# A macaron block in float32 on one core: y is normalised into a buffer in SBUF, GpSimd makes its low part, and the order of the work is written anew

## The chip, the cores and the metric

The kernel runs on one core of one Trainium2 chip. The metric is the device time of one execution in microseconds (us), the median over several executions. Less is better.

## The reference

x has 16 sequences of 1024 tokens with 512 channels. Three sublayers follow one another, each on the layer norm of its input:

```
x = x + 0.5 * ffn(layernorm(x))
x = x + attn(layernorm(x))
x = x + 0.5 * ffn(layernorm(x))

ffn(x):  s = x @ Win + bin                    # 512 -> 64
         h = relu(s[..., None] * W1 + b1)     # 64 -> 64 x 16
         g = sum(h * W2, -1) + b2             # back to 64
         return g @ Wout + bout               # 64 -> 512
attn(x): q, k, v = split(x @ w_attn)          # 16 heads of 32
         q, k = elu(q) + 1, elu(k) + 1
         S_t = S_{t-1} + k_t v_t^T;  z_t = z_{t-1} + k_t
         y_t = (q_t S_t) / (q_t . z_t + 1e-6)
         return y @ w_proj
```

## The kernel before, in words

The tokens are cut into NB = 32 blocks of 512, four tiles of 128 tokens each; two blocks make a sequence. Block j of the main loop does the attention of block j and, packed into the two halves of the partitions, the last feed-forward of block j-1 (half 0) and the first feed-forward of block j+2 (half 1). Blocks -2 and -1 before the loop and NB and NB+1 behind it are feed-forwards that run alone.

Products with large weights are made in three passes (`split3`): a float32 operand is a high part, rounded to the format that TensorE takes at full rate, and a low part, the rest. High parts are made by a copy on ScalarE (ACT), low parts by a subtraction, mostly on VectorE (DVE). For y, the attention's output, these are `yh` (ACT `ysplit`) and `yl` (DVE `ysplit`, in the helper at L931).

In a block the PE program is: `project` (k and q, 96 matmuls), `values`, `key` (a transpose of k), `den`, `ff_in`, and then for the four tiles t: `scores(t)` into the four PSUM banks `att`; ACT copies heads 0 and 2 into `A` and GpSimd (POOL) masks them, DVE masks heads 1 and 3 while it moves them; `attend(t)` adds the state's part (L1501) and the scores' part (L1510) into the same four banks; `update(t)` (L1521) makes the state's increment; DVE `ynorm(t)` divides y by its denominator in place in `att`; ACT and DVE split it; `outer(t)`, two times six matmuls with w_proj, gives what is added to x. `channels` transposes the next block's normalised input, and `ff_out` ends the two feed-forwards. `hidden` is one of 16 steps of a feed-forward's inner sum: a Relu on ACT, and a multiply and add on DVE.

Three things set the order. Each engine's program is a list written out by hand, and an engine runs its list strictly in order. Waits are on semaphores: `take` and `take_all` on PE wait until the bank they are given is free. And which bank a product gets is worked out by `give` when the program is built: the bank among those allowed that was given out longest ago, to be taken when `emptied` says so. ATT are banks 0 to 3 (`att`), RING is banks 5 to 7; bank 4 holds the feed-forward's sum. The banks of scores(t) come free, for scores(t+1) among others, with the semaphore `s_yl`: behind the last reading of y, the DVE subtraction.

Ahead of the loop the weights are loaded into buffers that are free then (`kT`, `qT`, `v`, `A`, `ktok`), and split by ACT and POOL. `s_walo` counts the low parts; DVE's first running sum of k (`zsum`, L1000) writes `A`, so it waits until w_proj's low part has been made from there.

## Time and profile before

| | |
|---|---|
| median of 3 runs | 2327.67 us (2326.47 to 2327.98) |
| the profiled execution: its time | 2329.01 us |
| its span in the trace | 2327.3 us |
| PE busy | 2266.8 us, 97% |
| DVE busy | 1935.2 us, 83% |
| ACT busy | 1438.7 us, 62% |
| POOL busy | 846.0 us, 36% |
| mean granted clock of TensorE | 0.989 |

Busy times are sums over an engine's instructions. A row of the timeline gives the start and the length of an instruction, or of several alike in a row (x4), and in brackets for how long the engine had been idle before it and who released it. PEld is TensorE's loading of weights, which overlaps its matmuls. Matmuls overlap one another, so the cost of one is best read as the distance of the starts.

### The profile page before, as it was taken

To read this page: it belongs to the slowest core of one execution; us is meant where nothing else is said; L and a number is where in the kernel's file an instruction comes from. 1 tells how busy PE (TensorE), PEld (TensorE's weight loads), DVE (VectorE), ACT (ScalarE), POOL (GpSimd) and SP (SyncE) were. 2 spreads that over 40 slices of the span, in tenths; PEclk is the share of its full clock that TensorE was granted. 3 is DMA by queue.
4 is the path that set the end of the run, shared out by engine and by line. 5 is a ranking of instruction groups with operands and counts; after the bars stand their busy time and mean duration, and the time that the engine had idled before them with its cause. 6 is when DMAs were issued, how large, how long until landed. Compare 5 with 4: busy or idle time off the path is not lost.

```text
span 2327.3 us, 74160 instructions
## 1 busy us (share of the span) xinstructions
PE 2266.8 (97%) x32210; PEld 1770.7 (76%) x32210; DVE 1935.2 (83%) x3393; ACT 1438.7 (62%) x2310; POOL 846.0 (36%) x871
## 2 busy tenths in 40 slices
PE   5899999999999999999999999999999999999997
PEld 3677777777777777777777777777777777777775
DVE  6888888889888889888889888889888889887767
ACT  6755657555657556657556656556656656666556
POOL 6333333433243433333333243434234333333312
PEclk8999999999999999999999999999999999999997
DMA  6001101111101111101111111111111111111111
GB/s 179 20 21 38 56 21 57 57 56 38 57 21 57 56 57 38 57 21 57 57 57 38 45 32 57 57 54 41 39 39 57 57 50 45 39 39 38 39 32 44
DMA packets 50215, 111.62 MB, mean 48 GB/s; under 512 B 8801, under 2 KB 10849, under 8 KB 45794
## 3 DMA queue, kind: packets, MB, share of 16 engines
q1 hardware_dynamic: 49890, 106.87, 15.1%
q8 instruction: 254, 4.16, 0.7%
q14 instruction: 71, 0.58, 0.1%
HBM read 72.25 MB, written 34.60 MB: 46 GB/s over the span
## 4 chain that ended last, share of the span: by engine, by line
PE 79%; DVE 13%; POOL 3%; issue 3%; ACT 2%; DMA 0%; DVEq 0%; SPq 0%; POOLq 0%; ACTq 0%
PE bank L1370 33%; PE att L1370 18%; PE att L1407 6%; PE att L1485 5%; PE att L1510 5%; PE att L1427 3%; DVE st L901 2%; DVE acc_psum L963 2%; PE att L1501 2%; PE bank L1436 2%; PE bank L1473 2%; POOL A L449 1%; DVE yl L931 1%; PE bank L1453 1%; DVE res L976 1%
## 5 line engine op out<-in xcount | busy, mean ns | idle before, releaser
L567 ACT ACTIVATE xhat<-res,nmr,rstd 128x512 f32<-128x512 f32 x384 | 298.4, 809 | 324.9 <-DVE nmr L909 266.7
L588 ACT ACTIVATE ffr<-ffs,b1c,w1c 128x512 f32<-128x512 f32 (+3 forms) x576 | 437.9, 781 | 27.9 <-DVE acc_psum L963 21.7
L453 POOL TENSOR_SCALAR_AFFINE_SELECT A<-A 128x512 f32<-128x512 f32 x256 | 156.6, 635 | 724.1 <-ACT A L540 724.1
L963 DVE SCALAR_TENSOR_TENSOR acc_psum<-ffr,w2c,acc_psum 128x512 f32<-128x512 f32 (+3 forms) x540 | 385.4, 714 | 32.4 <-ACT ffr L588 7.5
L442 POOL TENSOR_TENSOR res<-res,hbout 128x512 f32<-128x512 f32 x256 | 353.9, 1403 | 0.4 <-ACT xhat L567 0.4
L449 POOL TENSOR_TENSOR A<-qT,A 128x512 f32<-128x512 f32 x128 | 192.3, 1514 | 244.6 <-DVE zc L1005 102.2
L901 DVE BATCH_NORM_STATS2 st<-res 128x6 f32<-128x512 f32 x384 | 261.5, 681 | 9.5 <-DMA res<-in_L_attn_x_dram 3.7
L1370 PE MATMUL att<-xh,wa_h 128*128 128x512 f32 x648 | 260.4, 402 | 1.5 <-DVE xl L931 1.5
L1370 PE MATMUL att<-xh,wa_l 128*128 128x512 f32 x648 | 256.7, 396 | 0.0
L1370 PE MATMUL att<-xl,wa_h 128*128 128x512 f32 x648 | 256.7, 396 | 0.0
L1370 PE MATMUL bank<-wa_h,xh 128*128 128x512 f32 x512 | 218.7, 427 | 0.0
L1370 PE MATMUL bank<-wa_h,xl 128*128 128x512 f32 x512 | 202.8, 396 | 0.0
L1370 PE MATMUL bank<-wa_l,xh 128*128 128x512 f32 x512 | 202.8, 396 | 0.0
L540 ACT ACTIVATE A<-att 128x512 f32<-128x512 f32 x256 | 138.3, 593 | 90.9 <-PE att L1485 90.8
L415 POOL TENSOR_SCALAR nmr<-mv 128x4 f32<-128x4 f32 x93 | 21.2, 228 | 458.9 <-DVE mv L903 458.9
L1370 PE MATMUL bank<-wp_h,yh 128*128 128x512 f32 x384 | 171.3, 446 | 0.0
L1025 DVE TENSOR_TENSOR A<-att,tri 128x512 f32<-128x512 f32 x256 | 163.5, 680 | 0.1
L944 DVE STREAM_TRANSPOSE xf<-xhat 128x512 f32<-128x512 f32 x244 | 162.7, 686 | 0.9 <-ACT xhat L567 0.9
L1485 PEld LDWEIGHTS att<-qT,kT 32*128 32x128 f32 x4096 | 125.9, 186 | 38.2 <-DVE yl L931 26.0
L1485 PE MATMUL att<-qT,kT 32*128 32x128 f32 x4096 | 150.3, 283 | 3.6 <-DVE yl L931 3.3
L1370 PEld LDWEIGHTS att<-xh,wa_h 128*128 128x128 f32 x648 | 122.0, 188 | 41.4 <-issue 8.2
L1370 PE MATMUL bank<-wp_l,yh 128*128 128x512 f32 x384 | 152.5, 397 | 1.0 <-issue 1.0
(135 smaller groups left out, 5060.6 us busy)
## 6 DMA issues: line engine op xcount, KB each, us to landing
xf<-scratch SPq DMA_DIRECT2D x128, 256.0 KB, 4.3
res<-in_L_attn_x_dram SPq DMA_DIRECT2D x31, 1024.0 KB, 5.3
out_dram<-res SPq DMA_DIRECT2D x31, 1024.0 KB, 4.3
scratch<-rden SPq DMA_DIRECT2D x128, 8.0 KB, 1.7
res<-in_L_attn_x_dram SPq DMA_DIRECT2D x4, 256.0 KB, 3.7
kT<-in_L_attn_w_attn_dram SPq DMA_DIRECT2D x1, 1024.0 KB, 5.7
qT<-in_L_attn_w_attn_dram SPq DMA_DIRECT2D x1, 1024.0 KB, 9.6
v<-in_L_attn_w_attn_dram SPq DMA_DIRECT2D x1, 1024.0 KB, 12.0
```

The costliest lines, as they stand in the source:

```text
L442: eng.tensor_tensor(r[:, t, :], r[:, t, :], hbout[:, :], ALU.add).then_inc(s_bias[half], 1)
L449: eng.tensor_tensor(z[:, g, :], qT[:, g, :], z[:, g, :], ALU.mult).then_inc(s_zq, 1)
L453: eng.affine_select(out=A[:, h, :, :], in_=A[:, h, :, :], compare_op=ALU.is_ge, fill=0.0, base=0, pattern=[[0, 4], [1, P]], channel_multip ...
L567: eng.activation(xhat[t % 2][:, :], res[b % SLOTS][:, t, :], ACT.Identity, bias=nmr[:, n, b % 2, t:t + 1], scale=rstd[:, n, b % 2, t:t + 1 ...
L588: eng.activation(ffr[i % 2][p, w], ffs[p, w], ACT.Relu, bias=b1c[p, i:i + 1], scale=w1c[p, i:i + 1]).then_inc(s_hr, 1)
L901: eng.bn_stats(st[:, n, o, t, :], r[:, t, :]).then_inc(s_bn[n], 1)
L944: eng.transpose(xf[half][:, t, :, :].rearrange("p c i -> p (c i)"), xhat[t % 2][:, :]).then_inc(s_tr[half], 1)
L963: eng.scalar_tensor_tensor(psum[p, w], r[p, w], w2c[p, i:i + 1], psum[p, w], ALU.mult, ALU.add).then_inc(s_hm, 1)
L1025: eng.tensor_tensor(A[:, h, :, :], att[:, h, :].rearrange("p (g i) -> p g i", g=4), tri[:, :].unsqueeze(1).to_broadcast([P, 4, P]), ALU.mu ...
L1370: op = eng.matmul(o, l, r, start=first and i == 1, stop=final and i == n)
L1407: op = eng.matmul(att[M * n:M * n + M, r, 0:P], win[d, c, :], xf[n][d, :, c, :], start=c == 0, stop=c == C // D - 1)
L1485: op = eng.matmul(att[:, h, g * P:g * P + P], kT[d, g, w], qT[d, g, w], start=True, stop=True)
```

## The change

1. **y in SBUF.** `ynorm` writes into a new buffer `yn` (one, 128x512) and no longer in place. ACT's `ysplit` reads `yn` for the high part, POOL's new `ysplit` makes the low part as `yn` less high part; DVE's is gone. `ynorm(t)` waits in addition until the low part of the tile before has been made.
2. **Banks.** The scores' banks come free with `s_yn`, that is behind `ynorm`.
3. **Order in a block.** On PE `scores(1)` comes ahead of `values(3)`, and each `outer` comes about a tile later; the lists of ACT, DVE and POOL and the calls of `give` are written anew to go with it. POOL runs its four `zsum` together.
4. **Ahead of the loop.** The loads of the five small parameters (ten issues, each parameter into both halves of the partitions) go from SP's queue to ACT's; weights are loaded earlier and in another order; k's, q's and Wout's high parts are made by POOL; low parts are made in pieces of 128x512, so that norms come between them; bout is loaded into all partitions and halved by POOL, where a matmul and an ACT copy did that.
5. **Lone feed-forwards** use four half buffers for the Relu's output, where they had two.

```diff
+        yn = sb("yn", [P, 4, P])
...
-            return {"v": s_v, "xT": s_xTl, "y": s_x2, "sc": s_yl}[kind], 4 * b + i + 1
+            return {"v": s_v, "xT": s_xTl, "y": s_x2, "sc": s_yn}[kind], 4 * b + i + 1
...
             give_all("sc", j, 0)
-            give(RING, ("v", j, 2), ("up", j, 0), ("key", j, 1), ("v", j, 3))
+            give(RING, ("v", j, 2), ("up", j, 0), ("key", j, 1), ("xT", j + 1, 0))
             give_all("sc", j, 1)
-            give(RING, ("xT", j + 1, 0), ("y", j, 0), ("up", j, 1), ("key", j, 2))
+            give(RING, ("v", j, 3), ("key", j, 2), ("y", j, 0))
             give_all("sc", j, 2)
-            give(RING, ("y", j, 1), ("up", j, 2), ("xT", j + 1, 1))
+            give(RING, ("up", j, 1), ("up", j, 2), ("y", j, 1), ("xT", j + 1, 1))
             give_all("sc", j, 3)
-            give(RING, ("y", j, 2))
+            give(RING, ("xT", j + 1, 2), ("xT", j + 1, 3))
...
+            def ysplit(b, t):                                     # POOL
+                o = t % 2
+                e.wait_ge(s_yh, 4 * b + t + 1)
+                eng.tensor_tensor(yl[o][:, :, :], yn[:, :, :], f32(yh[o][:, :, :]), ALU.subtract).then_inc(s_yl, 1)
...
-                copy(yh[o][:, :, :], att[:, :, 0:P], s_yh)        # ACT
+                copy(yh[o][:, :, :], yn[:, :, :], s_yh)
...
                 e.wait_ge(s_num, 4 * b + t + 1)                   # DVE
                 e.wait_ge(s_rs, 64 * (b + 1))
-                eng.tensor_tensor(att[:, :, 0:P], att[:, :, 0:P], rs[:, :, t * P:t * P + P], ALU.mult).then_inc(s_yn, 1)
+                e.wait_ge(s_yl, 4 * b + t)
+                eng.tensor_tensor(yn[:, :, :], att[:, :, 0:P], rs[:, :, t * P:t * P + P], ALU.mult).then_inc(s_yn, 1)
...
-            def ysplit(b, t):                                     # DVE
-                o = t % 2
-                e.wait_ge(s_yh, 4 * b + t + 1)
-                lo_part(yl[o][:, :, :], att[:, :, 0:P], yh[o][:, :, :], s_yl)
...
-                e.wait_ge(s_hm, hid(j, i) - 2)
+                e.wait_ge(s_hm, hid(j, i) - (4 if alone(j) and i >= 2 else 2))
```

Three places in the middle of the loop show what moved. First PE, from `attend(1)` of a block to `attend(2)`. L1501 and L1510 are attend, L1521 is update, L1473 is key, L1485 is scores, wp_h and wp_l are outer. Before:

```order
L1501 MATMUL att<-qT,S 32x128 [waits s_ac1,s_am3,s_am1,s_ac0]
...
L1510 MATMUL att<-A,v 32x128 [waits s_am2,s_am0]
...
L1521 MATMUL bank<-v,ktok 32x32 [waits s_v]
...
L1370 MATMUL bank<-wp_h,yh 128x512
...
L1473 MATMUL bank<-ident,kT 128x128 [waits s_xTl]
...
L1485 MATMUL att<-qT,kT 128x128 [waits s_yl]
...
L1370 MATMUL bank<-wp_h,yh 128x512 [waits s_x2]
```

The same stretch in the changed kernel, where the lines are L1515 and L1524 (attend), L1535 (update) and L1499 (scores):

```order
L1515 MATMUL att<-qT,S 32x128 [waits s_ac1,s_am3,s_am1,s_ac0]
...
L1524 MATMUL att<-A,v 32x128 [waits s_am2,s_am0]
...
L1384 MATMUL bank<-wp_h,yh 128x512 [waits s_yl,s_xTl]
...
L1499 MATMUL att<-qT,kT 128x128 [waits s_yn]
...
L1535 MATMUL bank<-v,ktok 32x32 [waits s_v]
...
L1384 MATMUL bank<-wp_h,yh 128x512
```

Before, half of outer(0), update(1), the other half and a key stood between attend(1) and scores(2), and scores waited on `s_yl`; now only half of outer(0) stands there, scores waits on `s_yn`, and it is outer that waits on `s_yl`.

Second POOL, from the masks of tile 0 to those of tile 3 in a block (L453 is a mask, L442 adds the bias to x). Before:

```order
L453 AFFINE_SELECT A<-A 128x512 [waits s_ac1]
L442 TENSOR_TENSOR res<-res,hbout 128x512 x4
L453 AFFINE_SELECT A<-A 128x512 [waits s_ac0]
L453 AFFINE_SELECT A<-A 128x512 [waits s_ac1]
...
L415 TENSOR_SCALAR nmr<-mv 128x4 [waits s_ag1]
```

And in the changed kernel (L463 is a mask, L447 the bias, L459 the new low part):

```order
L463 AFFINE_SELECT A<-A 128x512 [waits s_ac0]
L463 AFFINE_SELECT A<-A 128x512 [waits s_ac1]
L459 TENSOR_TENSOR yl<-yn,yh 128x512 [waits s_yh]
L447 TENSOR_TENSOR res<-res,hbout 128x512 x2
L459 TENSOR_TENSOR yl<-yn,yh 128x512 [waits s_yh]
L463 AFFINE_SELECT A<-A 128x512 [waits s_ac0]
L463 AFFINE_SELECT A<-A 128x512 [waits s_ac1]
L447 TENSOR_TENSOR res<-res,hbout 128x512
L463 AFFINE_SELECT A<-A 128x512 [waits s_ac0]
L463 AFFINE_SELECT A<-A 128x512 [waits s_ac1]
L459 TENSOR_TENSOR yl<-yn,yh 128x512 [waits s_yh] x2
```

The low part of tile 0 stands behind the masks of tile 1, that of tile 1 behind two biases and ahead of the masks of tile 2, those of tiles 2 and 3 behind the masks of tile 3.

Third ACT in the changed kernel, from the low end of tile 1 to the norm of the next block's tile 1 (L561 is a copy, L609 a hidden, L588 a norm):

```order
L561 ACTIVATE yh<-yn 128x512 [waits s_po,s_yn]
L561 ACTIVATE A<-att 128x512 [waits s_sc0,s_num]
L609 ACTIVATE ffr<-ffs,b1c,w1c 128x512 [waits s_hm]
L561 ACTIVATE A<-att 128x512 [waits s_sc2]
L609 ACTIVATE ffr<-ffs,b1c,w1c 128x512 [waits s_hm]
L561 ACTIVATE ktok<-bank 128x512 [waits s_up,s_kt]
L588 ACTIVATE xhat<-res,nmr,rstd 128x512 [waits s_tr1]
```

Before, the two copies of the scores of tile 2 followed each other directly, as here:

```order
L540 ACTIVATE yh<-att 128x512 [waits s_po,s_yn]
L540 ACTIVATE A<-att 128x512 [waits s_sc0,s_num]
L540 ACTIVATE A<-att 128x512 [waits s_sc2]
L588 ACTIVATE ffr<-ffs,b1c,w1c 128x512 [waits s_hm]
L540 ACTIVATE ktok<-bank 128x512 [waits s_up,s_kt]
```

A `hidden` now stands between the two copies.

## Rows read from the trace of the kernel before

**Rows 1.** The page: the row of ACT's hidden, all forms together.
```profile
L588 ACT ACTIVATE ffr<-ffs,b1c,w1c 128x512 f32<-128x512 f32 (+3 forms) x576 | 437.9, 781 | 27.9 <-DVE acc_psum L963 21.7
```

**Rows 2.** Windows: busy time of each engine, instructions, PEclk, DMA share, GB/s.
```profile
0.00:41.00 41.00, 15.15 (x78) 9.88 (x78) 26.54 (x65) 23.31 (x35) 23.57 (x43) 0.79 0.83 247
41.00:130.00 89.00, 80.87 (x936) 62.27 (x936) 71.88 (x130) 60.29 (x94) 36.26 (x30) 0.94 0.07 17
1393.00:1463.00 70.00, 69.62 (x1014) 54.41 (x1014) 59.35 (x103) 43.22 (x69) 24.61 (x27) 1.00 0.16 48
```

**Rows 3.** Waits of PEld in one block, 1393 to 1463: total, times, longest.
```profile
PEld att L1485 <- DVE yl L931: 0.7, 3, 0.4
```

**Rows 4.** Timeline of PE in that block: attends, outers, scores, feed-forward's end.
```profile
1431.76 0.50 PE L1501 MATMUL att<-qT,S 32*32 32x128 f32 x32
...
1433.09 0.48 PE L1521 MATMUL bank<-v,ktok 128*32 128x32 f32 x32
...
1438.40 0.48 PE L1370 MATMUL bank<-wp_h,yh 128*128 128x512 f32 x1
...
1439.98 0.50 PE L1501 MATMUL att<-qT,S 32*32 32x128 f32 x32
...
1444.85 0.50 PE L1370 MATMUL bank<-wp_h,yh 128*128 128x512 f32 x1
...
1446.59 0.51 PE L1501 MATMUL att<-qT,S 32*32 32x128 f32 x32
...
1453.09 0.51 PE L1501 MATMUL att<-qT,S 32*32 32x128 f32 x32
...
1454.67 0.66 PE L1436 MATMUL bank<-ident,xhat 128*128 128x128 f32 x4
...
1460.23 0.50 PE L1427 MATMUL att<-wo_h,yh 64*128 64x512 f32 x2 [0.25 <-DVE yl L931]
```

**Rows 5.** Chain of waits of that block in order of time: start, us, what.
```profile
1396.45 5.60 PE bank L1370 x24
...
1448.18 0.71 DVE att L1018
...
1448.91 0.60 ACT yh L540
...
1449.54 0.69 DVE yl L931
```

**Rows 6.** Timeline of POOL, DVE and ACT in that block.
```profile
1431.36 5.05 POOL L442 TENSOR_TENSOR res<-res,hbout 128x512 f32<-128x512 f32 x4
...
1433.84 0.69 DVE L1018 TENSOR_TENSOR att<-att,xf 128x512 f32<-128x512 f32 x1
...
1444.99 1.09 ACT L540 ACTIVATE A<-att 128x512 f32<-128x512 f32 x2 [2.10 <-PE att L1485]
...
1445.66 1.22 POOL L453 TENSOR_SCALAR_AFFINE_SELECT A<-A 128x512 f32<-128x512 f32 x2 [5.63 <-ACT A L540]
```

**Rows 7.** Timeline of DVE: two running sums of one block.
```profile
1406.02 1.26 DVE L1000 TENSOR_TENSOR_SCAN A<-kT,zc 128x512 f32<-128x512 f32 x1
...
1410.20 2.07 DVE L1000 TENSOR_TENSOR_SCAN A<-kT,zc 128x512 f32<-128x512 f32 x1
```

**Rows 8.** Timeline of the start, 0 to 56 (SPq is SyncE's issuing of loads).
```profile
7.41 2.07 PE L1537 MATMUL att<-ktok,tri 1*128 1x512 f32 x2 [7.41 <-DMA ktok<-in_L_ffn_bout_dram]
...
6.43 1.24 SPq L357 DMA_DIRECT2D w1c<-in_L_ffn_W_dram  x2
...
18.32 0.63 ACT L540 ACTIVATE wo_h<-ktok 128x512 fp32r<-128x512 f32 x1
...
49.00 4.63 POOL L427 TENSOR_TENSOR wp_l<-A,wp_h 128x2048 fp32r<-128x2048 f32 x1
...
54.99 1.23 DVE L909 SCALAR_TENSOR_TENSOR nmr<-mv,rstd 128x4 f32<-128x4 f32 x1 [5.78 <-POOL rstd L417]
```

**Rows 9.** Timeline of the end: the last feed-forward's sum.
```profile
2314.23 6.78 DVE L963 SCALAR_TENSOR_TENSOR acc_psum<-ffr,w2c,acc_psum 128x128 f32<-128x128 f32 x15
```

More of the change, by code:

```diff
@@ L201, in carried, with relu_of @@
             return 4 * (b // PER * (PER - 1) + b % PER) + g + 1
+        def relu_of(j, i):
+            w = columns(j)
+            o = BLK // 2 * (i // 2 % 2) if alone(j) else 0
+            return ffr[i % 2][halves(j), w.start + o:w.stop + o]
         def hid(j, i):
@@ L369, in _ @@
             load(2)
-            wp_v = w_proj.rearrange("(g h e) n -> g e h n", g=4, h=4)
-            for g in range(4):
-                eng.dma_start(wp_st[D * g:D * g + D, :, :], wp_v[g]).then_inc(s_wp, 16)
             load(3)
@@ L499, in _ @@
                     rstds(L2, 1)
-                if on(j + 2):
-                    bias(1, j + 2, 2)
+                if on(j):
+                    mask(j, 1, 0)
+                    mask(j, 1, 2)
+                    ysplit(j, 0)
                 if on(j - 1):
@@ L504, in _ @@
                     bias(0, j - 1, 2)
[L505 removed]
                 if on(j):
[L507 to L508 removed]
+                    ysplit(j, 1)
                     mask(j, 2, 0)
@@ L1237, in _ @@
                 if on(j):
+                    mask(j, 3, 3)
+                    mask(j, 3, 1)
+                if on(j + 1):
+                    channels(j + 1, 1)
+                if on(j):
+                    outer(j, 1)
+                if j == NB - 1:
+                    var_of(L3, j, 1)
+                    shift_of(L3, j, 1)
+                if on(j):
                     ynorm(j, 3)
+                if on(j + 3):
+                    stats(L1, j + 3, 3)
                 if on(j - 1) or on(j + 2):
                     hidden(j, 15)
-                if on(j):
-                    ysplit(j, 3)
                 if on(j + 1):
@@ L1532, in outer @@
                     op.then_inc(s_po, 1)
-            e.wait_ge(s_bout, 16)
-            e.wait_ge(s_const, 7)
-            o = take("bout", 0, 0)
-            eng.matmul(o[:, :], tri[0:1, :], bout_st[0:1, :], start=True, stop=True).then_inc(s_mbout, 1)
             for t in range(TILES):
@@ L1590, in _ @@
                     key(j, 1)
-                    values(j, 3, 0)
-                    values(j, 3, 1)
-                    scores(j, 1)
                 if on(j + 1):
@@ L1596, in _ @@
                 if on(j):
+                    scores(j, 1)
+                    values(j, 3, 0)
+                    key(j, 2)
+                    values(j, 3, 1)
+                    attend(j, 1)
                     outer(j, 0, 0)
-                    attend(j, 1)
+                    scores(j, 2)
                     update(j, 1)
                     outer(j, 0, 1)
-                    key(j, 2)
-                    scores(j, 2)
-                    outer(j, 1, 0)
                     attend(j, 2)
                     update(j, 2)
-                    outer(j, 1, 1)
+                    outer(j, 1, 0)
                 if on(j + 1):
@@ L1617, in _ @@
                 if on(j):
-                    outer(j, 2, 1)
+                    outer(j, 1, 1)
+                    attend(j, 3)
                 if on(j + 1):
                     channels(j + 1, 3)
+                if j == NB - 1:
+                    flip(0, j, 0)
+                if on(j):
+                    outer(j, 2, 0)
+                    outer(j, 2, 1)
                 if j == NB - 1:
```

434 lines of the change are left out of this document (212 added, 222 removed).

## The prediction

> **What bounds the kernel now.** I read the windows first, then PE's waits and timeline inside one block, then the chain of waits, then the two ends. In the block from 1393 to 1463 PE is busy 69.6 of 70 us at a clock of 1.00, DVE 59.4, ACT 43.2 and POOL 24.6 [rows 2]. So the middle is bound by PE, and matmuls of full size follow one another every 5.60 / 24 = 0.233 us [rows 5]: nothing another engine does can make those faster. A change can win only what PE loses between them: waits, and the turns between full matmuls and small tiles. Six matmuls of outer are worth 6 x 0.233 = 1.40 us, but between small tiles they take 1439.98 - 1438.40 = 1.58 [rows 4], so a turn there and back costs 0.18. The two ends are different: in the first 41 us PE is busy for 15, and from 41 to 130, the first block, PE is busy 80.9 of 89 us at a clock of 0.94 [rows 2], against 70 us that a block takes later.
>
> **What PE loses in a block now.** Between attend(t) and scores(t+1) there is a chain, which the chain of waits shows: ynorm 0.71, high part 0.60, low part 0.69 on DVE, ACT, DVE [rows 5]. PE fills it, but not quite: three weight loads of scores wait 0.7 in all [rows 3]; loads overlap matmuls, so I count half, 0.35 (0.1 to 0.7). Before attend(2) the six matmuls of outer take 1446.59 - 1444.85 = 1.74 and not 1.58: 0.16 of waiting for the scores' copies and masks [rows 4]. attend(3) takes 1454.67 - 1453.09 = 1.58 where attend(0) takes 1433.09 - 1431.76 = 1.33: 0.25 more [rows 4]. The end of the feed-forwards waits 0.25 for its low part on DVE [rows 4]. Together 1.0 us in a block.
>
> **The middle, what the change takes away.** The bank's release moves two links up, behind ynorm: of the chain 0.60 + 0.69 and their hand-overs no longer stand ahead of scores. An outer comes a tile later, so its operands are mostly long ready. All four waits above can go: 1.0 us. The new order of PE also has one turn fewer (values(3) is cut by a key, but outer(2) and outer(3) run on together) and sets transposes side by side: I count 0.35 for both (0.2 to 0.5). DVE loses four subtractions of 0.69 a block, about 2.6 us of 59.4; that buys no time by itself, since DVE isn't the bound, but its queue is shorter by these where ynorm and outer stand. POOL's four zsum now run without a bias between them. That spares DVE a collision: the running sum takes 1.26 alone and 2.07 where it meets POOL's bias [rows 7]. It shortens the way to the denominators, for which PE waits a few tenths: 0.1 to 0.2. Sum of what is taken away: 1.0 + 0.35 + 0.15 = 1.5 us.
>
> **The middle, what it adds.**
> - scores(1) moves up, right behind update(0), key(1) and one `channels`. It needs ynorm(0). ynorm(0) now starts at 1433.84 and takes 0.69 [rows 6], and a release takes about 0.15 (scores end at 1444.85, the ACT copy starts at 1444.99 [rows 4, 6]): 1434.68, which is 1.59 behind the end of attend(0) at 1433.09 [rows 4]. PE has only the update (0.4, its row's 0.48 less the overlap) and eight transposes (0.65, the length of a row of four with its overlap) to do: 1.05. It waits 0.5. The `channels` wait inside the same gap for their norm.
> - ACT puts a hidden between the two copies of the scores of tile 2. The second copy, and POOL's mask behind it, come later by a hidden (0.78 [rows 1]) less its overlap and less what POOL had to queue anyway: 0.6. Before, PE waited 0.16 there; now it has an update more (0.4) to fill in. It waits 0.16 + 0.6 - 0.4 = 0.35.
> - The low part on POOL. No row shows this subtraction on POOL; the nearest are four biases in 5.05, 1.26 each, also two operands in SBUF and beside DVE's work on PSUM [rows 6]. For tile 0 it stands behind the masks of tile 1, which are 1.22 for two [rows 6] and follow ACT's copies; laid out from attend(0) it ends some 0.2 before PE reaches outer(0): no wait. For tile 3 the chain is ynorm, high part, low part, 0.71 + 0.60 + 1.26 and four hand-overs, 3.1 us, behind a DVE that has outer(1) and its statistics in front; PE has transposes and outer(2) to fill, 0.4 + 12 x 0.233 + 0.1 = 3.3. DVE starts ynorm(3) some 0.3 late, so PE waits 0.05 to 0.3; I take 0.1. The high part read from SBUF is 0.63 for 0.60 [rows 8, 5].
> - At the end of a block DVE has outer(3) and its statistics ahead of the first ff_out, whose bank the last PE ff_out takes; PE arrives there sooner than before: 0.1.
> Sum: 0.5 + 0.35 + 0.1 + 0.1 = 1.05. The block is shorter by 1.5 - 1.05 = 0.45 us; over 31 blocks 14 us.
>
> A rule that speaks against this: the Trainium skill, "GPSIMD Engine Reference", section 3.1, has elementwise work with two operands about twice as slow on GpSimd as on VectorE. The trace agrees, 1.26 against 0.69. Its section 8 says that the two share SBUF interfaces and get in each other's way when VectorE reads two operands from SBUF, and rows 7 show such a case. In the attend part DVE's instructions each read at least one operand from PSUM or have only one, so that by the rule too the price stays near 1.26.
>
> **The start.** PE's first flips stand behind bout's matmul, which waits for its load until 7.41 and takes to 9.4 [rows 8]. Without it they could start near 7. But ACT now issues ten loads first. No row shows an issue on ACT; the bounds are nothing, and 0.62 each as on SP (1.24 for two [rows 8]), 6 us, with which ACT's first norm comes at 8.3 and the feed-forward's input 1.1 earlier than now; with nothing it is 1.9. The copy of Wout (0.63) leaves the hidden loop: 0.55. The first projections at 41 start 1.6 earlier. In the first block DVE stands idle for 5.78 until 54.99, behind POOL, which makes w_proj's low part until 53.6 [rows 8]; now k's and q's parts are done early, w_proj's ends near 47.5 and DVE goes on 6 us earlier. The first block has about 10 us of PE waits (19 us more than a later one, less the lone feed-forward and 1 us of slow clock), nearly all for DVE. Of them 6 - 1.6 = 4.4 go, and I take 4. Start together: 5.5 (2 to 9). What could spoil it: ACT copies w_proj's high part ahead of the second norms, so a late load would stop it; its load is issued early enough by 2 to 3 us.
>
> **The end.** Four buffers for the Relu gain nothing where DVE's chain through one PSUM sum bounds: 15 steps in 6.78, 0.45 each [rows 9], each waiting for the one before. The last outers come later, DVE has less to do: 0.5 (-1 to 1.5).
>
> Sum: 14 + 5.5 + 0.5 = 20. The profiled execution took 2329.0 with a span of 2327.3, 1.3 above the median of the runs; I take the 20 off the median: 2308.
>
> **The rivals.**
> - *As worked out*, 2308, its own range 2297 to 2318: 0.50.
> - *Dense*: DVE's and ACT's shorter queues bring ynorm(0) and the second copy forward, and the new waits don't show. Then 1.3 us a block: 31 x 1.3 + 6 = 46, 2282. For it: the old waits all hang on the long chain. Against: ynorm(0) isn't behind anything now, it starts as soon as the update is added. 0.12.
> - *The new waits eat the middle*: waits as large as those removed (tile 1, tile 2 and the end of the block), only the start is won: 2317 to 2327, mid 2322. For it: every new gap above is a matter of 0.1 to 0.5. 0.20. The front going wrong as well as 14 won in the middle lands here too, 0.08 more.
> - *Slower*: POOL's low part is slow. If it costs 2.0 and not 1.26, outer(0) waits 0.55, the masks of tile 2 wait behind tile 1's low part, 0.3, and in tile 3 two of them stand in the chain, 1.0 more: 1.9 a block against 0.45 won, 31 x 1.4 = 45, less 6: 2366. It decides from about 0.26 more per subtraction, at 1.52. For it: rows 7 show that the two engines hold each other up. Against: the biases beside the same DVE work go at 1.26. 0.10.
>
> **The numbers.** No change that a measurement of this kernel can tell is within 0.2%, 4.7 us. Faster: 0.50 + 0.12 + 0.14 of the third + 0.07 = 0.83; the same 0.07; slower 0.10. The range leaves out most of the slow case and half of the dense one: 2286 to 2326.
>
> **What would show it.** A block of 69.5 us; no PE wait for yl ahead of scores; scores(1) waiting about 0.5 for DVE's yn; the second mask of tile 2 late by a third of a microsecond; POOL's yl near 1.26; first projections near 39.5 and DVE's wait for POOL in the first block gone. It would be wrong if yl on POOL is over 1.5, if outer waits for it in most tiles, or if ACT's issues are far from 0.6.

## The result

The changed kernel is slower. Its median is 2338.35 us (2336.45 to 2341.45), the one of before measured beside it 2327.19 (2326.47 to 2327.98): ratio 1.0043, 95% interval 1.0031 to 1.0055. The prediction was 2308, range 2286 to 2326. The profiled execution took 2336.85 us, its span is 2335.1. The two profiled executions therefore differ by 7.8 us where the medians differ by 11.2, and what follows explains the 7.8.

The windows of the kernel after, with the columns of [rows 2], show the same picture as before: PE full, at clock 1.00, in a middle block, less on DVE (55.96 for 59.35), more on POOL (29.35 for 24.61).

```profile
0.00:41.00 41.00, 13.43 (x78) 9.73 (x79) 27.24 (x67) 22.54 (x33) 33.73 (x56) 0.78 0.88 260
41.00:126.00 85.00, 78.77 (x937) 60.42 (x935) 68.89 (x126) 56.87 (x92) 36.55 (x38) 0.97 0.06 14
1254.00:1324.00 70.00, 69.65 (x1014) 54.23 (x1012) 55.96 (x97) 43.02 (x69) 29.35 (x30) 1.00 0.16 48
```

"PE busy 69.6 of 70" stands there in both kernels and can't tell a faster block from a slower one: a row of busy time holds waits inside a group of matmuls. So I cut PE's timeline at the starts of its groups. The first projection of the second block comes at 125.9 instead of 130.0 (4.1 earlier), the one of the last block at 2242.5 instead of 2233.1 (9.4 later), and from there to the end it takes 92.6 instead of 94.2. The start won 4.1, the end 1.6, and the thirty blocks between lost 13.5, 0.45 each. That this is the size that was forecast, with the other sign, is a coincidence.

The 4.1 is one execution of each kernel. The fifteen runs below share everything ahead of the loop, and in their profiles the first projection comes between 40.57 and 42.67 and that of the second block between 126.4 and 130.7 (the order inside the first block differs among them). So the start is known to a microsecond or two only.

From PE's timeline of one of these blocks in the kernel after (start, length, what; same columns as [rows 4]):

```profile
1292.99 1.10 PE L1524 MATMUL att<-A,v 128*32 128x128 f32 x32
1293.88 0.48 PE L1535 MATMUL bank<-v,ktok 128*32 128x32 f32 x32
1294.29 0.65 PE L1487 MATMUL bank<-ident,kT 128*128 128x128 f32 x4
1294.81 0.63 PE L1450 MATMUL bank<-ident,xhat 128*128 128x128 f32 x4
1295.37 1.17 PE L1499 MATMUL att<-qT,kT 32*128 32x128 f32 x32
...
1300.33 1.10 PE L1524 MATMUL att<-A,v 128*32 128x128 f32 x32
1301.44 0.50 PE L1384 MATMUL bank<-wp_h,yh 128*128 128x512 f32 x1
...
1304.53 0.50 PE L1384 MATMUL bank<-wp_h,yh 128*128 128x512 f32 x1
...
1306.29 0.51 PE L1515 MATMUL att<-qT,S 32*32 32x128 f32 x32
1306.93 1.08 PE L1524 MATMUL att<-A,v 128*32 128x128 f32 x32
...
1321.09 0.50 PE L1441 MATMUL att<-wo_h,yh 64*128 64x512 f32 x2
...
1323.58 0.50 PE L1441 MATMUL att<-wo_h,yh 64*128 64x512 f32 x2
```

From the update behind attend(0) to scores(1) it is 1295.37 - 1293.88 = 1.49; attend(1)'s A v part takes 1301.44 - 1300.33 = 1.11; the outer ahead of attend(2) takes 1306.29 - 1304.53 = 1.76, as long as before [rows 4], and behind it the state part takes 0.64 where attend(0)'s takes 0.43; from the first ff_out to the fourth it is 1323.58 - 1321.09 = 2.49. Ahead of 1321.09 there is no wait for the feed-forward's yl any more, as [rows 4] had.

The outer ahead of attend(2) is the first half of outer(1) in the kernel before and the second half of outer(0) in the changed one. Ahead of scores(2), behind attend(1), there stood update(1), one half of outer(0) and a key; the other half of outer(0) already came before attend(1).

Medians over the blocks 3 to 30, odd and even (an even block has no state part and no read of the state in tile 0, and has key(3) and update(3) at its end), each from the start of a group on PE to the start of the next. "start" is the run r1_start below, whose attention part is the one of before, to 0.02 everywhere; "r9" the kernel after with three places mended.

```
                                  odd blocks              even blocks
                               start  after   r9       start  after   r9
denominators                    1.01   1.01  1.01       1.01   1.01  1.01   (before: 1.21 and 1.26)
update(0) to scores(1)           -     1.49  1.43        -     1.92  1.43
attend(1), its A v part         0.90   1.11  1.03       0.90   1.11  1.08
outer ahead of attend(2)        1.74   1.76  1.60       1.74   1.76  1.59
state part of attend(2)         0.44   0.64  0.43       0.44   0.64  0.43
scores(3)                       1.10   1.11  1.27       1.10   1.10  1.27
state part of attend(3)         0.58   0.43  0.52       0.58   0.43  0.52
last outers (4 halves/3 in even)  -    5.88  6.12        -     4.39  4.62
four ff_out                     3.13   3.38  3.38       3.10   3.21  3.21
all groups, medians added      69.77  70.10 70.06      69.83  70.74 70.30
whole blocks, their mean       69.82  70.35 70.37      69.91  70.78 70.47
```

The groups' medians added up give a typical block (to 0.02). The last row is what was really spent: single blocks are longer than the typical one, and in odd blocks r9 is by that row no shorter than the kernel after.

### The profile page after: what moved, and what is told of

It reads as the page before. It is cut to its first block, busy times and chain, and to the rows that moved or that the text cites. A ratio compares the mean times of both kernels' runs of the same rounds, so it can differ in the third digit from the quotient of the medians.

```text
span 2335.1 us, 74420 instructions
## 1 busy us (share of the span) xinstructions
PE 2269.0 (97%) x32208; PEld 1763.6 (76%) x32208; DVE 1835.8 (79%) x3265; ACT 1429.6 (61%) x2307; POOL 995.3 (43%) x1014
## 4 chain that ended last, share of the span: by engine, by line
PE 89%; ACT 6%; issue 2%; DVE 2%; POOL 0%; DMA 0%; ACTq 0%; DVEq 0%; SPq 0%; POOLq 0%
PE bank L1384 36%; PE att L1384 23%; PE att L1421 6%; PE att L1499 5%; PE att L1524 5%; PE bank L1450 3%; PE att L1441 3%; ACT ffr L609 3%; PE att L1515 2%; PE bank L1441 1%; PE bank L1467 1%; PE bank L1487 1%; PE bank L1535 1%; ACT xhat L588 1%; ACT A L561 1%
## 5 line engine op out<-in xcount | busy, mean ns | idle before, releaser
L588 ACT ACTIVATE xhat<-res,nmr,rstd 128x512 f32<-128x512 f32 x384 | 304.8, 810 | 355.3 <-DVE nmr L929 251.4
L609 ACT ACTIVATE ffr<-ffs,b1c,w1c 128x512 f32<-128x512 f32 (+3 forms) x576 | 431.2, 777 | 6.7 <-DVE acc_psum L983 1.6
L463 POOL TENSOR_SCALAR_AFFINE_SELECT A<-A 128x512 f32<-128x512 f32 x256 | 158.5, 636 | 521.1 <-ACT A L561 521.1
L454 POOL TENSOR_TENSOR A<-qT,A 128x512 f32<-128x512 f32 x128 | 202.2, 1585 | 321.1 <-DVE zc L1025 151.9
L447 POOL TENSOR_TENSOR res<-res,hbout 128x512 f32<-128x512 f32 x256 | 324.4, 1288 | 2.2 <-ACT xhat L588 2.2
L459 POOL TENSOR_TENSOR yl<-yn,yh 128x512 fp32r<-128x512 f32 x128 | 165.1, 1290 | 91.5 <-ACT yh L561 91.5
L1499 PEld LDWEIGHTS att<-qT,kT 32*128 32x128 f32 x4096 | 125.9, 186 | 38.4 <-issue 20.0
L1499 PE MATMUL att<-qT,kT 32*128 32x128 f32 x4096 | 150.4, 283 | 3.3 <-DVE res L996 2.7
L561 ACT ACTIVATE A<-att 128x512 f32<-128x512 f32 x256 | 141.1, 590 | 19.6 <-PE att L1499 19.5
```

The source lines that it names most:

```text
L447: eng.tensor_tensor(r[:, t, :], r[:, t, :], hbout[:, :], ALU.add).then_inc(s_bias[half], 1)
L454: eng.tensor_tensor(z[:, g, :], qT[:, g, :], z[:, g, :], ALU.mult).then_inc(s_zq, 1)
L459: eng.tensor_tensor(yl[o][:, :, :], yn[:, :, :], f32(yh[o][:, :, :]), ALU.subtract).then_inc(s_yl, 1)
L561: eng.activation(dst, src, ACT.Copy).then_inc(done, 1)
L588: eng.activation(xhat[t % 2][:, :], res[b % SLOTS][:, t, :], ACT.Identity, bias=nmr[:, n, b % 2, t:t + 1], scale=rstd[:, n, b % 2, t:t + 1 ...
L609: eng.activation(relu_of(j, i), ffs[p, w], ACT.Relu, bias=b1c[p, i:i + 1], scale=w1c[p, i:i + 1]).then_inc(s_hr, 1)
```

## The experiments

Fifteen kernels ran. Their ratios are to the kernel before, measured beside them (its median went from 2328.30 to 2331.34 us between the four groups, so ratios are compared across groups and not times).

**First group: the parts one by one.** r1_start: start and front of the block as changed, everything from scores(0) on as before (VectorE makes the low part from the banks, the banks are released with it). r2_yn_dve adds only the buffer and the earlier release:

```diff
-            return {..., "sc": s_yl}[kind], 4 * b + i + 1
+            return {..., "sc": s_yn}[kind], 4 * b + i + 1
-                eng.tensor_tensor(att[:, :, 0:P], att[:, :, 0:P], rs[...], ALU.mult)
+                e.wait_ge(s_yl, 4 * b + t)
+                eng.tensor_tensor(yn[:, :, :], att[:, :, 0:P], rs[...], ALU.mult)
-                lo_part(yl[o][:, :, :], att[:, :, 0:P], yh[o][:, :, :], s_yl)
+                lo_part(yl[o][:, :, :], yn[:, :, :], yh[o][:, :, :], s_yl)
```

r3_yn_pool takes the four low parts from VectorE's list and puts them on GpSimd's, ahead of the masks of tiles 1, 2, 3 and behind those of 3. r4_after_dve_low is the kernel after with its four low parts back on VectorE, about where GpSimd had them.

> The kernel before with only the changed start (loads issued by ScalarE, weights' low parts in another order, bout without a matmul) and the changed front of a block (running sums ahead of the biases, denominators earlier); attention part, its buffers and the end as before. After its change the kernel reached its second block 4.1 us sooner and its denominators waited 0.2 us a block less. Theory (the loss lies in the attention part's order, start and front are gains): 2327.2 - 4.1 - 30 x 0.2 = 2317, range 2314 to 2320. Rival A (the front is part of the loss, its gain at the denominators is given back behind them): 2323 or more. Rival B (the start's 4.1 us is made by the new middle of the first block and not by the loads): 2320 to 2322.

> The first kernel of this call plus one thing: VectorE's ynorm writes the SBUF buffer yn, the four banks count as free with it, and VectorE makes the low part from yn; the order is that of before. It tests the prediction's first term alone. The prediction had 1.0 us a block of waits behind the banks' release, of which the scores' 0.35 and attend(3)'s 0.25 hang on the release: as predicted 30 x 0.6 = 18 us below the first kernel, near 2299. Theory from the trace of after (transposes followed by scores take 0.53 in both kernels whatever they wait for, so that little of this was waiting): 0 to 0.1 us a block, 2313 to 2318.

> The second kernel of this call with the low part on GpSimd (1.29 us each) in place of VectorE (0.69), in the order of before, where outer(3) stands 2.25 us behind attend(3) and the chain ynorm, high part, low part with GpSimd takes 3.1: PE waits about 0.6 to 0.8 a block there. Theory: slower than the second kernel by 30 x 0.5 to 0.8 = 15 to 24 us, of it nearly all at outer(3), none at outer(0) to outer(2). Rival (GpSimd's low part is dear everywhere, through VectorE's and GpSimd's queues): 30 us or more, with waits at outer(0) to outer(2) too. Rival (it is free, VectorE's relief pays for it): within 5 us.

> The changed kernel with one part undone: VectorE makes the low part (from yn), GpSimd doesn't; order, buffers and release as changed. Theory (the low part on GpSimd isn't what made the block longer; the order did, by the transposes of channels(0) waiting for their norm, by y(0)'s bank behind the overwriting of xh that waits for values(3), by a hidden between two copies): 2335 to 2345, the block within 0.15 us of 70.55. Rival (GpSimd's low part is the cause of the 0.45 us a block): 2322 to 2328, the block near 70.1 or less.

Measured: r1_start 2319.95 us, ratio 0.9953 (0.9940 to 0.9967); r2_yn_dve 2322.06, 0.9961 (0.9948 to 0.9973); r3_yn_pool 2340.01, 1.0037 (1.0024 to 1.0050); r4_after_dve_low 2361.47, 1.0128 (1.0114 to 1.0142).

So the start and the front are worth 11 us, the earlier release nothing that can be measured (the intervals overlap), and GpSimd's low part in the old order costs 18. The release was the first term of the prediction, and what it rested on is best read from one row of three kernels: the weight loads of all scores, total busy time and mean, then the idle time ahead of them by releaser.

Before:

```profile
L1485 PEld LDWEIGHTS att<-qT,kT 32*128 32x128 f32 x4096 | 125.9, 186 | 38.2 <-DVE yl L931 26.0 <-issue 11.6 <-DVE res L976 0.6
```

r2_yn_dve, where the bank is free two links earlier:

```profile
L1497 PEld LDWEIGHTS att<-qT,kT 32*128 32x128 f32 x4096 | 125.9, 186 | 37.1 <-issue 34.0 <-DVE res L990 3.1
```

After:

```profile
L1499 PEld LDWEIGHTS att<-qT,kT 32*128 32x128 f32 x4096 | 125.9, 186 | 38.4 <-issue 20.0 <-DVE yn L1039 15.3 <-DVE res L996 3.1
```

The idle time is 38, 37 and 38 us; only its label changes. (r1_start, from which r2_yn_dve differs by the buffer and the release alone, has 39.3: about 2 us in the whole kernel hung on the release.) Transposes with scores behind them take 0.53 in all three. So this was a gap of the loads' own, and the semaphore that came last in it was not what it waited for. At one place r2_yn_dve is slower than r1_start: channels(3) to outer(3) takes 0.47 for 0.36. No run took that apart.

In r3_yn_pool the loss that stays is at one place, PE's timeline of one block:

```profile
1319.43 0.60 PE L1442 MATMUL bank<-ident,xhat 128*128 128x128 f32 x4
1320.53 0.47 PE L1376 MATMUL att<-wp_h,yh 128*128 128x512 f32 x1 [0.51 <-POOL yl L460]
```

1.10 from the transposes to outer(3), 0.47 in r2_yn_dve and 0.36 in r1_start: tile 3 has no filling for a chain with 1.29 in it. In the kernel after both outer(2) halves stand there, and the wait is not seen. r4_after_dve_low held against the rival and went far past my own expectation: with its low parts on VectorE the new order costs 0.0085 more, 20 us. The outer ahead of attend(2) grows from 1.76 to 2.40, because VectorE now has a subtraction, besides the two masks that stand there in the kernel after too, ahead of the sum of update(1), which the state part reads; PE's timeline:

```profile
1322.30 0.51 PE L1524 MATMUL att<-qT,S 32*32 32x128 f32 x32 [0.73 <-DVE S L1059]
```

So with VectorE's list as it is the new order needs GpSimd for the low parts, and the old one must not have it in tile 3. Another place for VectorE's subtractions in the new order was not tried.

**Second group: mending the new order.** r5_chan_late puts the transposes of channels(j+1,0) behind values(3), where their bank and their xh can be written at once:

```diff
                     key(j, 1)
-                    channels(j + 1, 0)
+                    key(j, 2)
                     scores(j, 1)
                     values(j, 3, 0)
-                    key(j, 2)
                     values(j, 3, 1)
+                    channels(j + 1, 0)
                     attend(j, 1)
```

r6_pair puts ScalarE's hidden(12) behind the second copy of the scores of tile 2. r8_first has ynorm(0) ahead of update(0) on VectorE and the norm of (j+1,0) ahead of hidden(5) on ScalarE. r9_all has all of it.

> The changed kernel with the transposes of channels(j+1,0) behind values(3) and not ahead of scores(1), and key(2) joined to key(1) in their place. Theory (three new waits come from where these stand: in even blocks PE waits for their norm, key to channels 0.95 where 0.41 would do; in all blocks y(0) gets the bank whose xh may only be written behind values(3), attend(1) to outer 1.11 instead of 0.90; values(3) is no longer cut by a key): even blocks shorter by 0.6 to 0.8, odd by 0.1 to 0.4, attend(1) to outer(0) 0.90 again; ratio to the kernel before 0.9980 to 0.9995, where the changed kernel has 1.0043. Rival (scores(1) can't start earlier anyhow, ynorm(0) bounds it, and y(0) has another wait behind this one): at most 0.15 a block, ratio 1.0025 to 1.0045.

> The changed kernel with one thing undone: ScalarE makes the two copies of the scores of tile 2 one after the other, the hidden(12) comes behind them. Theory (this hidden between them makes PE wait ahead of attend(2), outer 1.76 + attS 0.64 against 1.58 + 0.43 without waiting): 0.2 to 0.35 a block, 6 to 11 us, ratio 1.0000 to 1.0020. Rival (the mask on VectorE or GpSimd or the accumulation's bank bounds attend(2), not the copy): under 0.08 a block, ratio 1.0035 to 1.0045.

> The changed kernel with two queue places swapped: VectorE takes ynorm(0) ahead of the update's sum, which waits for a later PE instruction, and ScalarE the norm (j+1,0) ahead of hidden(5). Theory: the norm is what even blocks wait for (key to channels 0.95 becomes 0.5 or less), ynorm(0) behind the update's sum is what odd blocks wait for (update to scores(1) 1.08 becomes 0.85 to 0.95); what stands behind keeps its waits (attend(1) to outer(0) grows, since y(0)'s bank waits for values(3) alone and not for these: no growth beyond 0.05). Even -0.4 to -0.5, odd -0.1 to -0.25, ratio 1.0005 to 1.0020. Rival (what is won here is lost at y(0)'s bank, at scores(2) or attend(2), which come from VectorE's and ScalarE's queues): ratio above 1.0030.

> The changed kernel with all three: channels(j+1,0) behind values(3), the two copies together, ynorm(0) and the norm first. Theory (all waits that the new order made are named): the sum of the three, 0.8 to 1.2 a block below the changed kernel, block 69.4 to 69.8, ratio 0.9895 to 0.9945, faster than the kernel with only the start changed (0.9953). Rival (each wait hides another of nearly its size): block 69.9 or more, ratio 0.9955 or more.

Measured: r5_chan_late 1.0012 (1.0003 to 1.0021), r6_pair 1.0056 (1.0043 to 1.0068), r8_first 1.0015 (1.0006 to 1.0024), r9_all 1.0014 (1.0005 to 1.0023). r5_chan_late falls between my theory and its rival, r6_pair is worse than both of its own, r8_first is as its theory said, and of r9_all the rival held.

The waits ahead of scores(1) were real. In the kernel after, an even block, PE stands for ScalarE's norm, which stands behind a copy and a hidden, PE's timeline and ScalarE's:

```profile
940.67 0.66 PE L1487 MATMUL bank<-ident,kT 128*128 128x128 f32 x4
941.62 0.63 PE L1450 MATMUL bank<-ident,xhat 128*128 128x128 f32 x4 [0.29 <-ACT xhat L588]
```

```profile
939.49 0.59 ACT L561 ACTIVATE v<-bank 128x512 f32<-128x512 f32 x1
939.97 0.81 ACT L609 ACTIVATE ffr<-ffs,b1c,w1c 128x512 f32<-128x512 f32 x1
940.67 0.81 ACT L588 ACTIVATE xhat<-res,nmr,rstd 128x512 f32<-128x512 f32 x1
```

Key to channels takes 0.95 there. r8_first brings it to 0.49, and the typical even block from 70.74 to 70.28; in odd blocks it wins 0.08. r5_chan_late wins the same 0.46 in another way and 0.07 in odd ones. In the mean of whole blocks the two win 0.26 and 0.28 in even blocks and 0.22 and 0.20 in odd ones. I had also expected 0.21 from y(0)'s bank; attend(1)'s part goes from 1.11 to 1.03 only, 0.08, and 1.03 is what it takes wherever no update follows.

r6_pair is the instructive miss. Of the wait ahead of attend(2) 0.23 went, within what I expected (1.76 + 0.64 became 1.59 + 0.58), and the time didn't go with it: the last outers grew from 5.88 to 6.12 and attend(3)'s state part from 0.43 to 0.52. In r9_all the two mended places ahead of scores(1) and the one at attend(2) together give 1.0014, no more than one of the first two alone.

In typical blocks r9_all loses at tile 3 (0.24 + 0.17 + 0.09 = 0.50 in odd blocks) more than attend(2) gave (0.38). The rest of its loss is scattered over single blocks. In eleven blocks VectorE now waits for something that was hardly ever waited for before (0.3 us, once, in r1_start), its waits in the middle of r9_all (total, times, longest):

```profile
DVE yn L1037 <- DMA xf<-scratch: 5.4, 11, 1.0
```

It is the readback of the denominators' reciprocals, which ynorm(0) multiplies by. In one block SyncE issued its four transfers from 1635.71 for 1.69 us, and ynorm(0) waited for them until 1643.38. In r1_start scores(1) stands 0.41 + 0.41 + 2.97 = 3.8 us behind attend(0) and hides a late transfer, here 1.4. Little of the 5.4 reaches PE, though; its own waits in that stretch are:

```profile
PE bank L1484 <- issue: 1.7, 2, 0.9
PE att L1496 <- DVE yn L1037: 1.0, 2, 0.5
```

The second row is the readback: blocks 22 and 28 are 0.5 to 0.6 longer by it. The first is in the two longest blocks, 23 and 25, 71.46 and 71.15 us, where PE stands for a key and waits for nothing that the trace shows, and VectorE for no readback:

```profile
1715.67 0.66 PE L1484 MATMUL bank<-ident,kT 128*128 128x128 f32 x4 [0.75 <-issue]
```

The kernel after has such a stop in the same block 23, at 1719.20, for 0.85. Its cause is open.

**Third group: what stays of a removed wait.** r10_sums_first takes r1_start and swaps two steps on VectorE, `sums(j)` ahead of `channels(j + 1, 3)`. r11_stats_late also moves outer(3)'s statistics behind the first ff_out of both halves. r12_last_of_after has the changed kernel's last block besides. r13_yn3_first is r9_all with

```diff
-                    outer(j, 1)
                     ynorm(j, 3)
+                    outer(j, 1)
```

> The kernel with only the start changed, and on VectorE the feed-forward's low part (sums) ahead of channels(j+1,3). It asks whether a PE wait that the trace names as PE's own can be had. There PE waits 0.26 to 0.42 in odd blocks for this low part (outer(3) 3.31 for twelve matmuls, of which 2.97 is work), 0 in even ones, where the update fills. Theory (the one real wait of the kernel before, but VectorE's first ff_out comes behind outer(3)'s statistics, so that the fourth ff_out's bank is as late as before): the segment with outer(3) shrinks by 0.34 and the one of ff_out grows by 0.25, as in the changed kernel; 0.1 in odd blocks, ratio 0.9945 to 0.9955. Rival (the wait is simply gone): 0.35 in odd blocks, 5 us, ratio 0.9925 to 0.9935.

> The kernel before this one, and outer(3)'s statistics behind the first ff_out of both halves on VectorE. Theory: with both, neither wait is left, 0.35 in odd blocks and 0.05 to 0.15 in even ones, 6 us: ratio 0.9915 to 0.9935, ff_out's segment 3.0 to 3.1. Rival (the bank of the fourth ff_out hangs on something else, such as outer(3)'s own bank): as the kernel before this one.

> The kernel before this one with the last block in the changed kernel's order, with yn and GpSimd's low part in that block alone. From the start of the last block to the end the changed kernel takes 88.7 us, the kernel with only the start changed 89.9; the block's attention part in the new order costs some 0.4 of it more. Theory (the end of the change is a gain of its own): 1.2 us below the kernel before this one, 0.5 to 2. Rival (the end was shorter only because the blocks ahead of it left their work further behind or ahead): within 0.4 us.

> The changed kernel with the three changes of the run before (channels late, copies together, ynorm(0) and the norm first), and on VectorE ynorm(3) ahead of outer(1) and its statistics. With the copies together the last four outers grew from 5.88 to 6.12 in odd blocks: theory (ynorm(3) stands behind outer(1)'s statistics, and GpSimd's low part behind it, so PE waits at outer(3)): 5.7 to 5.85 and 4.3 to 4.4 instead of 4.62 in even ones, 0.25 to 0.4 a block, ratio 0.9960 to 0.9985. Rival (VectorE only waits itself for attend(3), and what stands behind comes later by as much: the banks of channels and the first ff_out): ratio 1.0005 to 1.0020.

Measured: r10_sums_first 0.9959 (0.9947 to 0.9972), r11_stats_late 0.9952 (0.9940 to 0.9965), r12_last_of_after 0.9946 (0.9934 to 0.9959), r13_yn3_first 1.0180 (1.0166 to 1.0194).

The wait ahead of the first ff_out in r1_start is a true one; PE's timeline:

```profile
1032.09 0.50 PE L1438 MATMUL att<-wo_h,yh 64*128 64x512 f32 x2 [0.26 <-DVE yl L945]
```

Followed through odd blocks by medians it goes like this:

```
                        outer(3)   four ff_out   24 x 4 projections   groups added
r1_start                  3.31        3.13            22.50           69.77
r10_sums_first            2.99        3.44            22.50           69.76
r11_stats_late            2.99        3.00            22.86           69.73
```

Whole blocks are 69.82, 69.85 and 69.82 in the mean. 0.32 gone at outer(3) comes back as 0.31 in the ff_outs; 0.44 gone there comes back as 0.36 in the next block's projections, whose bank VectorE's ff_out frees. That part I had expected to be won (0.9915 to 0.9935). PEld's waits in the middle of r11_stats_late have a row that r1_start has not:

```profile
PEld bank L1384 <- DVE res L990: 11.8, 28, 0.5
```

At the end of a block VectorE is behind, with two outers, their statistics and the first ff_outs; PE waits for it somewhere, and each edit chooses where. The kernel after fits this: it lost the wait for the feed-forward's yl and got 0.25 more in its ff_outs.

r13_yn3_first shows the same with a price. The last outers went from 6.12 to 5.77, as expected of ynorm(3) being late. But VectorE then stands idle for attend(3), and outer(1), whose bank channels(3) takes, comes behind it; PE's timeline:

```profile
1335.81 1.08 PE L1522 MATMUL att<-A,v 128*32 128x128 f32 x32
1338.36 0.66 PE L1448 MATMUL bank<-ident,xhat 128*128 128x128 f32 x4 [1.47 <-DVE res L1062]
```

0.35 won, 1.01 made 2.55 and so 1.54 lost in each block. I had named this as the rival, but with a ratio of 1.0020 at most.

r12_last_of_after: from the last block's start to its last matmul 88.7 us and not 90.5, as the kernel after has it; 1.8 us in the profile, 1.4 in the medians (2317.30 and 2318.72), with intervals that overlap.

**Fourth group: what was still open.** r14_pool_three is r3_yn_pool with tile 3's low part on VectorE, r15_tile3_dve is r9_all with the same, r16_best is r12_last_of_after with the buffer and GpSimd's low part for tiles 0 to 2.

> Start as changed, order as before, banks released with yn, low part on GpSimd for tiles 0 to 2 and on VectorE for tile 3. With all four on GpSimd it was 1.0037, with none 0.9961. Theory (GpSimd's low part costs only where the chain is short of filling, tile 3): back to 0.9950 to 0.9970, channels(3) to outer(3) 0.35 to 0.48 again and not 1.10. Rival (the load on GpSimd's queue or on the port costs by itself): a third or more of the 18 us stays, 0.9985 or more.

> The kernel with all three undone (1.0014), with VectorE making the low part of tile 3. Theory (what stays of the loss is tile 3's chain with 1.29 in it, which ends behind outer(2)): the last four outers 5.8 to 5.9 and not 6.12 in odd blocks, 4.35 to 4.45 and not 4.62 in even ones, 0.2 a block, ratio 0.9980 to 0.9995. Rival (VectorE's queue is the chain there, ynorm(3) is late and a subtraction more on it makes the rest later): no gain or a loss, ratio 1.0010 or more.

> The fastest so far (0.9946: start and last block as changed, order of before, sums first, statistics late) with yn and GpSimd's low part for tiles 0 to 2. Theory (PE's waits at the block's end come from VectorE's queue there, which the relief in tiles 0 to 2 doesn't reach, since VectorE has waits of its own between): within 2 us of it, 0.9940 to 0.9955. Rival (VectorE's queue carries its lateness through the block, and 1.8 us less of it brings the block's end forward): the projections' segment 22.5 and not 22.86 in odd blocks, 0.15 to 0.35 a block, ratio 0.9900 to 0.9930.

Measured: r14_pool_three 0.9958 (0.9944 to 0.9972), r15_tile3_dve 1.0015 (1.0007 to 1.0024), r16_best 0.9948 (0.9936 to 0.9961).

The 18 us of r3_yn_pool are tile 3's alone: with it back on VectorE they are gone, though GpSimd still makes three of four. In the new order GpSimd's 1.29 in tile 3 isn't what PE waits for: r15_tile3_dve has 6.13 at the last outers, r9_all 6.12, against my theory and for its rival. VectorE's ynorm(3) is, as r13_yn3_first showed. And VectorE's relief by three subtractions a block is worth nothing in the old order (0.9948 against 0.9946).

The fastest kernels are r12_last_of_after and r16_best, 0.9946 and 0.9948, not to be told from r11_stats_late or r1_start by their intervals. All of them are faster than both kernels of this study, and nearly all of it is the start and the front.

## Why the prediction was wrong

By its own steps, odd blocks where nothing is said.

1. *"Three weight loads of scores wait 0.7 in all ... I count half, 0.35."* Wrong, the failed step. It was no waiting: r2_yn_dve took the release away from the chain and kept 37 of 38 us of idle loads (39 in r1_start) and 0.53 for each pair. [rows 3] names the last semaphore, and I took that for a cause. Counting half was no caution, since nothing in the row said that any of it depended on the release.
2. *Outer before attend(2), 0.16.* Not won: 1.76 for 1.74. With the copies together it is (1.60), so the term had the right size, and the added hidden kept it.
3. *attend(3), 0.25.* 0.13 came: the state part 0.58 to 0.43, the A v part 1.01 to 1.03, which is its length wherever no update follows. Comparing it with attend(0), which an update follows, made 0.12 of waiting out of nothing.
4. *End of the feed-forwards, 0.25.* Won at its place and lost behind it: 0.25 in the ff_outs. r10_sums_first and r11_stats_late moved the same wait twice more without a gain.
5. *Turns, 0.35.* Hardly there. All outers of a block take 12.31 instead of 12.72, but 0.32 of that is item 4's wait, which stood in the last of them; and values(3), cut by a key, takes 1.50 + 1.58 for 2.97.
6. *Denominators, 0.15.* Right, 0.20 in odd and 0.25 in even blocks. The row that names it in the waits of the kernel before, `PEld bank L1453 <- POOL A L449`, has no successor after.
7. *scores(1) waits 0.5 for ynorm(0).* The total was right in odd blocks, 1.05 + 0.5 = 1.55 for 1.49, its parts were not: 0.41 + 0.41 + 0.53 = 1.35 of it PE takes for the update, the key and the transposes whenever nothing is late, so that 0.14 is waiting. In even blocks it took 1.92, 0.57 of waiting. I had written that the transposes wait for their norm inside the same gap and given that no price; without a state part PE arrives 0.43 earlier, and the norm does not.
8. *attend(2), 0.35.* Right: 0.38 went in r9_all, 0.23 in r6_pair. But it could not be had back by taking the hidden away.
9. *Low part on GpSimd.* Right: 1.29 for 1.26, and about 0.1 at outer(3). The row of the kernel after:

```profile
L459 POOL TENSOR_TENSOR yl<-yn,yh 128x512 fp32r<-128x512 f32 x128 | 165.1, 1290 | 91.5 <-ACT yh L561 91.5
```

The Trainium skill ("GPSIMD Engine Reference", section 3.1) has work on two operands about twice as slow on GpSimd; the trace agrees, 1.29 for VectorE's 0.69. By its section 8 the Trainium skill has the two engines contend for shared SBUF interfaces beside VectorE instructions with two inputs in SBUF or in a 2-port mode; no slowing shows in this part of the block, where 1290 is the mean of 128.

10. *ff_out's bank, 0.1.* 0.25, with item 4.
11. *Start 5.5 (2 to 9).* 4.1 in the profile, 2.6, 3.4 and 2.8 in the first three runs, which share it: in the lower half of the range. ScalarE's issues took the 0.62 each of the upper bound, and its first norm came at 8.49 for the 8.3 forecast, behind a table load that before lay in idle time. What I had missed is what stands behind that norm; PE's and ScalarE's timeline of the kernel after:

```profile
7.20 1.28 ACT L588 ACT_TABLE_LOAD   x1 [7.20 <-issue]
8.49 1.52 ACT L588 ACTIVATE xhat<-res,nmr,rstd 128x512 f32<-128x512 f32 x2
9.36 3.74 PE L1392 MATMUL att<-ident,xhat 128*128 128x128 f32 x16 [9.36 <-ACT xhat L588]
10.57 1.67 ACT L588 ACTIVATE xhat<-res,nmr,rstd 128x512 f32<-128x512 f32 x2 [0.56 <-PE att L1392]
```

PE's first flips come at 9.36 (before 9.41), and the third norm waits for them and comes at 10.57 (before 10.63). So the feed-forward's input is 0.4 earlier and not 1.1, and the first projection, at 40.42 for 41.25, 0.8 and not 1.6. VectorE's wait of 5.78 for GpSimd in the first block is gone (longest now 1.9), as said, but VectorE now waits there for ScalarE's q, 5.3 us in two waits, which the forecast of 4 us did not have.

12. *End 0.5.* 1.6, and 1.8 by r12_last_of_after.

The sum, against r1_start, which has the denominators' 0.2 already: the typical block is longer by 0.33 in odd blocks (70.10 - 69.77) and 0.91 in even ones (70.74 - 69.83), 0.62 on average. From the second block's start to the last one's it is 20.6 us, 0.69 a block; the 0.07 on top are blocks longer than the typical one. Forecast without the denominators was 1.05 - 1.35 = -0.30. The difference of 0.99 a block is 30 us in thirty blocks. The profiled pair is 27.8 us off the forecast, 7.8 longer instead of 20 shorter: against those 30 the denominators gave 2.6 and the end 1.1 more than forecast, and the start 1.4 less. On the side of what is taken away, 0.13 and some 0.07 came in odd blocks (attend(3), and what the ff_outs left of the feed-forward's wait), 0.2 for 1.35: short by 1.15. What was added is what remains, some 0.8 to 0.9 for 1.05. So the added side was even priced a little high, and the removed side was a label, a comparison of unlike neighbours, a wait that VectorE hands on, and turns that another turn paid for. Of my rivals "the new waits eat the middle" was the nearest, with 0.28; that they would eat more than the middle's gain while GpSimd subtracts at 1.29 was in no case, since I had tied the slower one to a slow GpSimd.

What is shown and what is argued: that release and GpSimd's speed are not the cause is shown by r2_yn_dve, r14_pool_three (tiles 0 to 2, in the old order) and r15_tile3_dve (tile 3, in the new one); that the waits ahead of scores(1) cost about 0.45 in even blocks by r5_chan_late and r8_first. That VectorE's queue sets what stays in tiles 2 and 3 is shown for tile 3 by r13_yn3_first, and argued for tile 2. Not settled: what makes ynorm(3) late in the typical block of r9_all, since no run took VectorE's queue there apart, and the stops of PE in blocks 23 and 25.

## What to carry to other kernels

A releaser behind idle time names the event that came last, not a cause. Before such a wait is counted as winnable, find the same pair of neighbours in the trace where the releaser is long done (here transposes before scores: 0.53 with `issue` as well), and compare an instruction only with one that has the same neighbours.

Where PE looks full, another engine can still be the local bound for a few microseconds of a period; a wait for it that is removed comes back at its next product. Follow a removed wait through the next three products of that engine before you book it, and take back first the work that has no deadline there.

A filler serves one wait. What moves values(3) behind scores(1) to cover tile 1's masks uncovers ynorm(0), the norm of the next block and, for two blocks in r9_all, a DMA readback, all of which its own 2.97 us had covered.

## What the runs showed that I had not expected

A table load of 1.28 us goes with the first activation in ScalarE's program, so issues placed ahead of it push it out of time in which the engine was idle anyway.

The readback of the denominators arrives about 6 us behind its last issue in some blocks (issued to 1637.40, waited for until 1643.38) and in others earlier; its spread shows only when it has no cover, and then mostly on VectorE: 5.4 us of waiting there, 1.0 on PE.

With the biases out from between the running sums both the biases and VectorE's sums are faster. GpSimd's addition of bout's half to the residual takes 1.40 on average before; in r1_start, where only the start and the front are changed, it takes 1.29, as in the kernel after:

```profile
L442 POOL TENSOR_TENSOR res<-res,hbout 128x512 f32<-128x512 f32 x256 | 353.9, 1403 | 0.4 <-ACT xhat L567 0.4
L448 POOL TENSOR_TENSOR res<-res,hbout 128x512 f32<-128x512 f32 x256 | 323.6, 1290 | 2.7 <-ACT xhat L581 2.7
```

VectorE's running sums go from 1.60 on average to 1.27 between the same two kernels:

```profile
L1000 DVE TENSOR_TENSOR_SCAN A<-kT,zc 128x512 f32<-128x512 f32 x64 | 102.3, 1598 | 0.6
L1014 DVE TENSOR_TENSOR_SCAN A<-kT,zc 128x512 f32<-128x512 f32 x64 | 81.4, 1272 | 0.6
```

GpSimd's own running sums, now one behind the other, are slower, 1.585 for 1.514 on average. The 0.20 to 0.25 a block at the denominators go with all this. That the collision with the biases is the reason is argued from [rows 7] and these means; the front was changed as a whole and no run took it apart.
